# Turning squares of 32 on VectorE and placing them by transfers, in a gated cross-attention block with a feed-forward part, on one Trainium2 core

## The reference, cut to what matters

```python
    # attention
    q = jnp.einsum('bsd,ed->bse', x, wq)
    k_new = jnp.einsum('bsd,ed->bse', x, wk)
    v_new = jnp.einsum('bsd,ed->bse', x, wv)
    k = jnp.concatenate([k_cache, k_new], axis=1)
    v = jnp.concatenate([v_cache, v_new], axis=1)
    scores = jnp.einsum('bqd,bkd->bqk', q, k) * scale
    attn = jax.nn.softmax(scores, axis=-1)
    out = jnp.einsum('bqk,bkd->bqd', attn, v)
    return jnp.einsum('bqd,ed->bqe', out, wo)
...
    # feed-forward, weights by their sign, 512 -> 2048 -> 512
    hidden = jnp.einsum('bsd,hd->bsh', x, up_w) * up_scale
    hidden = jax.nn.relu(hidden)
    out = jnp.einsum('bsh,dh->bsd', hidden, down_w) * down_scale
...
    x = x + jnp.tanh(g_xattn[0]) * _L0_xattn_ref(_layernorm(x, axis=-1), mask_BxSx4224_bf0, ctx_2048, ctx_2048, ...)
    x = x + jnp.tanh(g_ffn[0]) * _L0_ffn_ref(_layernorm(x, axis=-1), ...)
```

## Time and profile before

| what | value |
|---|---|
| median of 3 runs | 594.27 us (594.06 to 594.32) |
| the profiled execution's own time | 593.66 us |
| its span, first to last instruction | 591.9 us |
| granted TensorE clock | 1.000 |
| TensorE matmul busy | 585.9 us (99%) |
| VectorE busy | 376.3 us (64%) |
| ScalarE busy | 289.0 us (49%) |
| GpSimd busy | 116.9 us (20%) |

### The profile page before, as it was taken

How to read it: one execution, slowest core, us unless ns; L and a number is a source line. 1 busy time by engine, 2 the same in 40 slices (tenths; PEclk the granted TensorE clock), 3 DMA queues, 4 the chain that set the end, 5 groups by cost and what they waited for, 6 DMA issues and landing times.

```text
span 591.9 us, 7100 instructions
## 1 busy us (share of the span) xinstructions
PE 585.9 (99%) x2738; PEld 487.6 (82%) x2738; DVE 376.3 (64%) x532; ACT 289.0 (49%) x426; POOL 116.9 (20%) x111
## 2 busy tenths in 40 slices
PE   8999999999999999999999999999999999999997
PEld 7888888888888888888888888888888888888885
DVE  5889454687543677534677786755458834766654
ACT  3875421555230655230656565655659445645531
POOL 5006303011003021003020025242322003342001
PEclk9999999999999999999999999999999999999999
DMA  8613121212020233020122222121110302230011
GB/s 291 246 51 143 41 72 66 70 37 72 1 72 0 66 148 107 1 71 2 71 71 72 79 69 102 37 71 35 63 46 35 126 17 73 85 130 37 0 72 71
DMA packets 20097, 43.21 MB, mean 73 GB/s; under 512 B 4832, under 2 KB 4832, under 8 KB 19680
## 3 DMA queue, kind: packets, MB, share of 16 engines
q1 hardware_dynamic: 20064, 42.76, 21.1%
HBM read 36.45 MB, written 6.30 MB: 72 GB/s over the span
## 4 chain that ended last, share of the span: by engine, by line
PE 97%; DVE 2%; DMA 0%; ACT 0%; issue 0%
PE proj L559 35%; PE score L693 19%; PE turn L678 12%; PE score L592 9%; PE score L559 7%; PE proj L678 5%; PE proj L592 4%; PE score L828 2%; PE turn L551 1%; PE score L551 1%; PE turn L661 1%; PE proj L661 1%; DVE rows L1670 1%; DMA rows<-in_x 0%; DVE probsT L1217 0%; DVE scaled L1667 0%
## 5 line engine op out<-in xcount | busy, mean ns | idle before, releaser
L693 PE MATMUL score<-down_signs,hid_split 128*128 128x512 f32 x512 | 133.4, 390 | 0.0
L693 PEld LDWEIGHTS score<-down_signs,hid_split 128*128 128x128 f32 x512 | 95.9, 188 | 20.5 <-DVE hid_split L1550 0.5
L559 PE MATMUL proj<-probsT,four_x 128*128 128x512 f32 x384 | 89.2, 391 | 0.0
L559 PEld LDWEIGHTS proj<-probsT,four_x 128*128 128x128 f32 x384 | 71.5, 188 | 14.5
L559 PE MATMUL proj<-four_x,weights 128*128 128x512 f32 x336 | 76.8, 389 | 0.0
L559 PEld LDWEIGHTS proj<-four_x,weights 128*128 128x128 f32 x336 | 63.0, 188 | 13.0
L484 POOL TENSOR_TENSOR four_x<-raw_ctx,four_x 128x2048 fp32r<-128x2048 f32 x7 | 32.6, 4655 | 189.2 <-ACT four_x L916 189.2
L924 ACT ACTIVATE four_x<-proj 128x512 fp32r<-128x512 f32 x32 | 19.0, 595 | 73.7 <-PE proj L559 73.7
L1222 DVE TENSOR_TENSOR four_x<-proj,four_x 128x512 fp32r<-128x512 f32 x32 | 22.1, 690 | 51.0 <-ACT four_x L924 51.0
L1550 DVE TENSOR_TENSOR hid_split<-hid,hid_split 128x512 fp32r<-128x512 f32 x64 | 44.4, 696 | 15.5 <-ACT hid_split L1135 15.3
L678 PE MATMUL turn<-ops_b,up_ops 128*128 128x512 f32 x192 | 51.7, 391 | 0.0
(11 more groups left out here) (132 smaller groups left out, 859.2 us busy)
## 6 DMA issues: line engine op xcount, KB each, us to landing
raw_w<-in_ffn_w SPq DMA_DIRECT2D x24, 512.0 KB, 3.2
raw_ctx<-in_ctx_turned SPq DMA_DIRECT2D x4, 1024.0 KB, 5.4
raw_ctx<-in_ctx SPq DMA_DIRECT2D x4, 1024.0 KB, 5.8
result<-rows SPq DMA_DIRECT2D x16, 256.0 KB, 2.0
rows<-in_x SPq DMA_DIRECT2D x3, 1024.0 KB, 5.5
turned_x<-in_x_turned SPq DMA_DIRECT2D x3, 1024.0 KB, 5.2
rows_away<-rows SPq DMA_DIRECT2D x1, 2048.0 KB, 14.7
rows<-rows_away SPq DMA_DIRECT2D x1, 2048.0 KB, 7.8
```

The source lines that it names most:

```text
L559: last = pe.matmul(bank, lhs(l), rhs(r), start=start and i == 0, stop=stop and i == 2)
L693: last = pe.matmul(wide(r), hid_split[:, n % HR, s, r * P:(r + 1) * P], down_signs[:, chunk_of(q), :], start=(q == 0 and s == HI), stop=(q ...
```

## The change

Two uses of TensorE's transposes are replaced.

The feed-forward rows: all 16 row tiles are normalized by DVE and turned by DVE in squares of 32x32 (`turn_squares`: `dve.transpose` turns each square inside itself). `store_squares` then writes a batch's four tiles to a DRAM tensor `block_rows` by four transfers, each square at the place where the whole turned matrix has it, and `block_rows_back` loads the batch, 1 MB, into `raw_x`. The tiles of batches 0 and 1 are turned in the batches 1 and 2 (`turn_pair_squares`), those of batches 2 and 3 in the groups `j` = 1 to 4 of the feed-forward part (`turn_late_squares`). `turn_block_rows`, its 64 transposes and ACT's 16 copies are gone. The order of the signs changes too: four blocks of the down weights are taken in the groups 0 to 3, ahead of the relu.

The probabilities: of each batch one row tile, `SQUARED = TILE_ORDER[0]` (tile 2), is turned by DVE in squares (`square_probs`, 128x1024 at once), and 16 transfers within the chip (`place_squares`) put the squares, in runs of 128 bytes, into `squares_placed`, which is the low half of `probsT`. ACT copies the high part from there (`placed_out`), DVE subtracts (`placed_low`). TensorE's turning jobs go from eight to six a batch, in runs of three.

```diff
-    TURNS_BATCH = 2 * RT
+    TURNS_BATCH = 2 * (RT - 1)
...
-        TURN_ORDER = ((2, NEW), (3, NEW), (0, NEW), (1, NEW), (2, OLD), (3, OLD), (0, OLD), (1, OLD))
+        TURN_ORDER = ((3, NEW), (0, NEW), (1, NEW), (3, OLD), (0, OLD), (1, OLD))
+        SQUARED = TILE_ORDER[0]
+        RUN = RT - 1
...
+            def store_squares(b, squares):
+
+                sp.wait_ge(block_turned, RT * (b + 1))
+                for i in range(P // SQ):
+                    sp.dma_start(squares_v[b, i], squares[i * SQ:(i + 1) * SQ].rearrange(
+                        "a r (j n) -> a r j n", n=SQ)).then_inc(squares_out[b], 16)
+
+            def place_squares(b):
+
+                sp.wait_ge(probs_squared, b + 1)
+
+                sp.wait_ge(scored, product_scored(b, A22, 1))
+                groups = probs_squares.rearrange("p (c k n) -> p k c n", c=KC, n=SQ)
+                for k in range(P // SQ):
+                    for i in range(P // SQ):
+                        col = SQUARED * P + i * SQ
+                        sp.dma_start(squares_placed[k * SQ:(k + 1) * SQ, :, col:col + SQ],
+                                     groups[i * SQ:(i + 1) * SQ, k]).then_inc(placed, 16)
...
+            for n in range(4, signs_at("up", 4)):
+                load_signs(n)
+            store_squares(2, late_squares)
+            load_signs(signs_at("down", 7) - 1)
+            load_signs(signs_at("up", 5) - 1)
+
+            sp.wait_ge(rows_spilled, 16)
+            block_rows_back(2)
+            load_signs(signs_at("up", 6) - 1)
+            load_signs(signs_at("up", 7) - 1)
+            store_squares(3, late_squares)
+            block_rows_back(3)
...
-                pe.wait_ge(turn_lo, turn0(b) + RT)
+                pe.wait_ge(turn_lo, turn0(b) + RUN)
+                pe.wait_ge(placed_lo, 2 * b + 1)
...
                     if e == 0:
-                        pe.wait_ge(turn_lo, turn0(b) + 2 * RT)
+                        pe.wait_ge(turn_lo, turn0(b) + 2 * RUN)
+                        pe.wait_ge(placed_lo, 2 * b + 2)
...
+            def placed_out(b, side):
+                part = (slice(None), slice(4 * side, 4 * side + 4), slice(SQUARED * P, (SQUARED + 1) * P))
+                act.wait_ge(placed, PLACED * (b + 1))
+                act.activation(probsT[:, HI][part], squares_placed[part], ACT.Copy).then_inc(placed_hi, 1)
...
                 proj_out(m + 2, new_side[:, HI, 2, :])
+                placed_out(b, NEW)
+                placed_out(b, OLD)
...
+            def square_probs(b):
+                dve.wait_ge(exp_done, tile_done(b, SQUARED))
+                dve.wait_ge(scored, product_scored(b, S2, 1))
+                dve.transpose(probs_squares[:, :], probs[:, SQUARED, :]).then_inc(probs_squared, 1)
...
+            def turn_squares(f, tile_normed, squares):
+
+                dve.wait_ge(block_rstd_done, f // RT + 1)
+                dve.tensor_scalar(tile_normed, rows[:, f, :], block_mean_var[:, f % RT, 0:1],
+                                  block_rstd[:, f % RT:f % RT + 1], ALU.subtract, ALU.mult).then_inc(block_normed, 1)
+                dve.wait_ge(block_normed, f + 1)
+                dve.transpose(squares, tile_normed).then_inc(block_turned, 1)
...
+            def turn_late_squares(f):
+
+                if f == 3 * RT:
+                    dve.wait_ge(squares_out[2], STORED)
+                for i in (f, f + 1):
+                    turn_squares(i, late_normed[:, i % 2, :], late_squares[:, i % RT, :])
...
                 maxima(b, 3)
+                square_probs(b)
                 maxima(b, 0)
...
-                if g == 0:
-                    take_signs(HG + 1)
                     act.wait_ge(x_ready, 7)
+                if g < len(LATE_DOWN):
+                    take_signs(signs_at("down", LATE_DOWN[g]) - 1)
...
-                if j in (1, 2):
-                    norm_stats(3 * RT + 2 * j - 2, 2)
+                if j in (1, 2, 3, 4):
+                    turn_late_squares(2 * RT + 2 * j - 2)
                 if j == 2:
-                    norm_moments(BATCH + 3)
+                    block_row_stats(3 * RT)
+                    block_row_moments(3)
```

More of the change, by code:

```diff
@@ L231, in gated_block @@
         signs_ready, left_ready = sem("signs_ready"), sem("left_ready")
-        raw_out, rows_spilled, rows_back = sem("raw_out"), sem("rows_spilled"), sem("rows_back")
+        rows_spilled, rows_back = sem("rows_spilled"), sem("rows_back")
+        block_stats_done, block_moments, block_eps, block_rstd_done = map(sem, (
+            "block_stats_done", "block_moments", "block_eps", "block_rstd_done"))
+        block_normed, block_turned = sem("block_normed"), sem("block_turned")
+        probs_squared, placed, placed_hi, placed_lo = map(sem, ("probs_squared", "placed", "placed_hi", "placed_lo"))
+        squares_out = [sem(f"squares_out{f}") for f in range(BATCH)]
+        block_in = [sem(f"block_in{b}") for b in range(BATCH)]
         new_read, half_out = sem("new_read"), sem("half_out")
@@ L424, in _ @@
                     sp.dma_start(raw_ctx[:, :, :], ctx_turned_v[b + 1]).then_inc(ctx_in, 16)
+                if b in (1, 2):
+                    store_squares(b - 1, pair_squares)
             sp.wait_ge(scored, product_scored(BATCH - 1, S3, 1))
-            for n in range(HG + 11):
+            for n in range(3):
+                load_signs(n)
+            place_squares(BATCH - 1)
+            load_signs(3)
+            sp.wait_ge(turned, TURNS_ALL)
+            block_rows_back(0)
+            block_rows_back(1)
+            for n in range(4, signs_at("up", 4)):
+                load_signs(n)
+            store_squares(2, late_squares)
[7 more added lines that the diff above has]
+            block_rows_back(3)
+            for n in range(signs_at("up", 8) - 1, HG + 11):
                 load_signs(n)
@@ L650, in v_jobs @@
                         pe.wait_ge(score_sums, 10 * (b + 1))
-                        for i in range(RT):
+                        for i in range(RUN):
                             turn_probs(b, i)
                     if r == 3:
-                        for i in range(RT, 2 * RT):
+                        for i in range(RUN, 2 * RUN):
                             turn_probs(b, i)
-            def turn_block_rows(f, bank):
-                pe.wait_ge(normed_done, RT + f + 1)
-                for k, tile in enumerate(cols(normed[:, f % RT, :])):
-                    last = pe.transpose(bank[:, k * P:(k + 1) * P], tile, ident[:, :])
-                last.then_inc(turned, 1)
-            def turn_two(f):
-                for i in (f, f + 1):
-                    if i < 2:
-                        pe.wait_ge(turn_lo, TURNS_ALL + i - 1)
-                    else:
-                        pe.wait_ge(raw_out, i - 1)
-                    turn_block_rows(i, turn[:, i % 2, :])
             def up_product(g, k, bank, left, i, start, stop):
@@ L707, in up_group @@
                 pe.wait_ge(signs_ready, signs_at("up", g))
-                if pair == 0 and j - 1 in TURNED_IN:
-                    pe.wait_ge(raw_out, TURNED_IN[j - 1] + 2)
                 if g == 0:
@@ L738, in up_group @@
                 piece(2)
-                if pair == 0 and j in TURNED_IN:
-                    pe.wait_ge(raw_out, TURNED_IN[j] + 1)
-                    turn_block_rows(TURNED_IN[j] + 1, proj[:, (g + 1) % 2, :])
                 pe.wait_ge(p1_out, g + 1)
@@ L1014, in take_signs @@
                 act.activation(dst, raw_w[:, :], ACT.Sign).then_inc(signs_ready, 1)
[L1016 to L1024 removed]
             def right_high(pair, i):
                 if i in (B11, B21):
[L1028 removed]
+                    act.wait_ge(block_in[2 * pair], 16)
                 elif i == B22:
[L1030 removed]
+                    act.wait_ge(block_in[2 * pair + 1], 16)
                 else:
@@ L1278, in sum_scores @@
                 bank = score[0 if k in (AT_P17, AT_C21) else 1][:, t, :]
+                if k == AT_P17 and t == 0 and b >= 2:
+                    dve.wait_ge(squares_out[b - 2], STORED)
                 if k in (AT_P17, AT_P16):
@@ L1298, in probs_out, with placed_low @@
                 turn_out(turn0(b) + i, lambda s: probsT[:, s, 4 * side:4 * side + 4, t * P:(t + 1) * P])
+            def square_probs(b):
+                dve.wait_ge(exp_done, tile_done(b, SQUARED))
+                dve.wait_ge(scored, product_scored(b, S2, 1))
+                dve.transpose(probs_squares[:, :], probs[:, SQUARED, :]).then_inc(probs_squared, 1)
+            def placed_low(b, side):
+                part = (slice(None), slice(4 * side, 4 * side + 4), slice(SQUARED * P, (SQUARED + 1) * P))
+                dve.wait_ge(placed_hi, 2 * b + (1 if side == NEW else 2))
+                dve.tensor_tensor(probsT[:, LO][part], squares_placed[part], probsT[:, HI][part].bitcast(F32),
+                                  ALU.subtract).then_inc(placed_lo, 1)
             def keys(b):
@@ L1430, in batch @@
                 proj_out(b, 1, chunk(new_side, 1))
```

(8 more changed lines are left out.)

137 lines of the change are left out of this document (65 added, 72 removed).

## The result

The changed kernel takes 605.48 us, median of 5 runs (603.91 to 606.7); the kernel before, on the same chip, 594.08 (593.88 to 594.32). The ratio is 1.0193, 95% interval 1.0181 to 1.0205: slower by 1.9%, and outside the predicted range of 584 to 598. The profiled execution took 605.48 us, its span is 603.4, 11.5 more than in the earlier trace rows.

What follows compares the result with a forecast made beforehand. TensorE was taken as the bound: 10.8 us of transposes removed, less 1.95 and 3.5 us of new waits in the groups, gave 5.4 us less, 588.3 us for the profiled execution, median 588.9, range 584 to 598.

Steps and rivals of the forecast that it cites:

- What bounds the kernel: Whole kernel: TensorE, busy 585.9 of 591.9 us, bounds it, so every new wait of TensorE is paid in full.
- What is removed: 96 TensorE transposes at 0.109 us: 3.5 us in the batches, 3.5 in the last batch, 3.8 in the groups; 10.8 together.
- VectorE's squares: DVE's turns in squares: 1.17 us for 128x1024 in a batch, 0.65 for 128x512 in the feed-forward groups.
- The spacing of issues ... I take 0.46: Each batch's 16 placing transfers on SP: issued 0.46 us apart, the last at 235.95 and placed at 237.95.
- The placement costs nothing: Each batch: squares placed at 237.95 against a limit of 239.1, 1.2 us of room, hidden by the third and fourth value job.
- the placement comes late: Rival, in the batches: SP issues at 0.70 us, the last square lands 2.45 late, four times: 598.7 us; chance 0.23.
- 0.46 without a full queue: Argument against late placement: issues were 0.46 us apart with little on the rings, 0.70 with megabytes queued.
- The last batch is alike, only that a load of signs stands behind the 16: Batch 3's placement: taken to cost nothing, as in the other batches, with a load of signs issued after it.
- only loads with time to spare: SP's queue in a batch: behind the 16 placing transfers stand only loads that are not urgent.
- The groups: Feed-forward groups: P5 at group 3 is 1.95 us late for DVE's sum, a block of signs 3.5 late at group 4.
- the slow stores: Rival, feed-forward groups: at 25 ns a packet 595.3 us; if only their landing is late, 592.3; slow or late together 0.20.
- the two late cases: Placement late, 0.23, 590 to 599 us, and stores slow or late to land, 0.20, 592 to 605.

Runs made afterwards that it cites:

- rows_free: Feed-forward part alone (all probability jobs on TensorE), order of loads, stores and statistics mended, batch 3's squares written to other memory: 585.99 us, 0.9869 of the kernel before.
- half_packets: The changed kernel with the same 16 placing transfers, each of 128 packets in place of 256: 602.79 us, ratio 1.0165 to the kernel before.
- via_hbm: The changed kernel with the probability squares placed by way of HBM, five issues in place of 16: 594.98 us, ratio 1.0024 to the kernel before.
- placed_in_order4: both_swapped with the 16 placing transfers within the chip in place of the way by HBM: 596.0 us, ratio 1.0032 to the kernel before.
- signs_between: The changed kernel with batch 3's load of signs issued between the 8th and 9th placing transfers: 603.6 us, ratio 1.0166 to the kernel before.
- both_swapped: The changed kernel with placement by HBM, order mended, batch 3's squares in other memory, batch 0's placement ahead of a 1 MB load: 583.91 us, ratio 0.9836.
- rows_mended: Feed-forward part alone (all probability jobs on TensorE), with three places of SP's and VectorE's order changed: 588.75 us, ratio 0.9924 to the kernel before.
- two_queues: The changed kernel with the last 4 of 16 placing transfers issued from POOL's queue, each in two halves: 637.74 us, ratio 1.0739 to the kernel before.

## Why the prediction was wrong

It was 16.6 us too low. By its own steps:

- **What bounds the kernel**: right. Every new wait of TensorE was paid in full, and more: 15.1 us of waits cost 23.0.
- **What is removed**: 10.8 said, 11.3 measured (3.5 in the batches, 4.04 in batch 3, 3.8 in the groups; the last two by `rows_free`). The 0.109 us of a transpose held; between batch 3's attention products there was 0.5 us more to win.
- **VectorE's squares**: right. The rows of 128x1024 last 1.23 us where 1.17 was taken, those of 128x512 0.71 where 0.65 was.
- **"The spacing of issues ... I take 0.46"**: this step failed, and with it "The placement costs nothing". The transfers come 0.65 us apart (0.61 each and 0.04 between), so the last one starts 9.8 us behind the first in batch 3, and 11.1 in batch 1, where 15 x 0.46 = 6.9 was worked out. The row taken was the gap between two transfers of other kinds (0.37 of issuing, then 0.45); the other bound, 0.70, was nearer. The 1.9 us from issue to landing were right (2.0 said), and the limit was near: with 0.65 the prediction's own sum gives 229.05 + 9.75 + 2.0 = 240.8, 1.7 late, and batch 2, for which it was worked out, waits 1.77. The rival "the placement comes late" is what happened, down to the second wait at the old half. It had 2.45 a batch, 9.8 us in four. Batches 0 to 2 paid 2.45 + 4.59 + 2.29 = 9.3, of which 6.4 are waits at the attention's start. `half_packets` (the same spacing), `via_hbm` (10.5 us back) and `placed_in_order4` (12.1 us) show issuing as the cause. The argument "0.46 without a full queue" was wrong: in batch 1 the DMA engines' share was 0.27.
- **"The last batch is alike, only that a load of signs stands behind the 16"**, and with it "only loads with time to spare": failed too. ACT needs that block ahead of the fourth value job's copy. Batch 3 paid 5.8 us. `signs_between` moved that load alone: the wait of 1.37 us is gone, and the median is 1.9 lower.
- **The groups**: both waits came, in place and in size (1.69 and 3.42 for 1.95 and 3.5). The way to the second was partly another: SP took 4.41 us to issue the four stores, which was counted at nothing, and the load took 5.55 us to land, where "2.2 us behind" the stores was said. The stores' data held as priced: the DMA engines work on it from about 404 to 411, some 7 us where 6.4 were worked out. On the clock of before (5.41 us earlier at group 3) it landed at 407.8, where 407.1 was said. What was missing is what comes beside the waits: 5.45 us said, 7.9 measured, and nearly all of the 2.4 between is the clock in group 4.
- **The clock** has no term in the prediction at all. Behind three of the waits it was 0.72, 0.66 and 0.67 in the windows above; in group 4 alone that is 15.80 - 9.97 - 3.42 = 2.4 us, and in batch 1 1.9. That it needs the waits is seen in that the low stretches go with them (`both_swapped`: the page gives TensorE 99% busy, and the granted clock is 1.000), not by an experiment on the clock itself; that a wait alone doesn't settle it is seen in `half_packets`.
- **The rivals**: the slow stores did not come (two waits, not three), but their landing did as soon as the rest was mended (`rows_mended`). Half of the 0.43 given to the two late cases is 0.22, not the 0.24 written.

The sum of the misses: 9.3 (batches 0 to 2) + 5.8 (batch 3) + 2.4 (the groups) - 0.5 (transposes) = 17.0 us, for 16.6.

## What to carry to other kernels

A transpose by squares moves work from TensorE to the queue that issues the transfers. Count transfers there first, at the time of one in a row of its kind (0.65 us here), and everything that stands behind them on that queue. Where 16 transfers do what five can, try the five even if they carry more packets and go by HBM: that was worth 12.1 us here. And before giving an edit up, look at the order around it: the same two parts are 605.5 us in one order and way of placing, and 583.9 in another.

## What the runs showed of the hardware

- Issuing a small transfer from SBUF to SBUF costs SP 0.60 to 0.61 us (median) whether it has 128 or 256 packets. In batches 1 and 2 the longest of the 16 takes 0.9 to 1.8; why isn't shown. Four of 2,048 packets of 128 bytes take 0.60, 1.00, 1.69 and 1.00 us, and four of 1,024 take 2.77 us together, 5.5 with a load of 1 MB on the rings.
- POOL's queue issued transfers of 128 packets mostly 2.0 us apart, and up to 6.1 (`two_queues`). The Trainium skill, page DMA: Bandwidth & Descriptors, section Issuing engines are not separate DMA queues, says that issuing from several engines only saves issue time, and that this is usually small beside the transfer. Here the trace differs on the second point: 16 issues took 10.4 to 11.7 us beside 1.9 of landing, and the second engine, POOL, saved nothing but cost 32 us.
- A transpose in squares on DVE takes 1.23 us for 128x1024 and 0.71 for 128x512, about what a maximum (1.22) and a subtraction (0.68) over the same shapes take.
- What comes back by HBM (four stores, one load) is placed 9.4 us after the first issue, with 3.9 us from the load's issue to its landing; 16 transfers within SBUF, each landing 1.9 us after its issue, take 13.0 (batch 1).
- TensorE's granted clock in the 4 us behind a new wait in a busy stretch: 0.53 to 0.61 in windows of 2 us (157 to 161) behind 2.71 us, 1.00 behind 1.92, 1.77 and 1.69; and 1.00 behind 2.63 in `half_packets`, but 0.50 in the window from 248 behind 2.21 in `signs_between`. Where it fell, 96 matmuls took 23.6 us for 22.3.
